# First unit of pairs 0 to 2: four of its eight transposed slots go through DRAM and VectorE instead of TensorE

## The reference

```python
hn = group_norm(x, gn1_scale, gn1_bias)
qkv = jnp.einsum('bchw,oc->bohw', hn, w_qkv) + b_qkv[None, :, None, None]
qkv = qkv.reshape(b * NHEAD, 3 * ch, n)
q, k, v = jnp.split(qkv, 3, axis=1)
scale = ch ** (-0.25)
wgt = jax.nn.softmax(jnp.einsum('bct,bcs->bts', q * scale, k * scale), axis=-1)
a = jnp.einsum('bts,bcs->bct', wgt, v).reshape(b, c, h, w)
out = jnp.einsum('bchw,oc->bohw', a, w_proj) + b_proj[None, :, None, None]
return x + group_norm(out, gn2_scale, gn2_bias)
```

## Time and profile before

| what | value |
|---|---|
| median of 3 runs | 3375.3 us (3374.86 to 3377.05) |
| the profiled execution, its own time | 3375.88 us |
| its span, first to last instruction | 3373.7 us |
| granted TensorE clock | 1.000 of full |
| PE busy | 3351.2 us, 99% |
| DVE, ACT, POOL busy | 63%, 55%, 32% |

### The profile page before, as it was taken

One profiled execution on the slowest core, in us unless ns is written; L12 is line 12 of the kernel. 1 busy time (PEld: TensorE's weight loads), 2 busy tenths in 40 slices (PEclk: granted clock), 3 DMA queues, 4 the chain that ended last, 5 costly groups with the idle time before them and its releaser, 6 DMA issues.

```text
span 3373.7 us, 51950 instructions
## 1 busy us (share of the span) xinstructions
PE 3351.2 (99%) x16816; PEld 2777.5 (82%) x16816; DVE 2132.7 (63%) x3489; ACT 1838.7 (55%) x3094; POOL 1064.3 (32%) x947
## 2 busy tenths in 40 slices
PE   8999999999999999999999999999999999999999
PEld 6888888888888888888888888888888888888887
DVE  5677357773578745786457854578555784557844
ACT  4677227862378523784337842388333882347822
POOL 1344104441045410453104531145211452124511
PEclk9999999999999999999999999999999999999999
DMA  8522244313534125331253212442224422343212
GB/s 340 149 67 59 79 131 124 93 34 94 140 99 101 62 57 151 103 86 76 53 167 91 73 75 76 144 101 63 93 61 144 98 63 94 92 139 70 63 57 75
DMA packets 109871, 332.15 MB, mean 98 GB/s; under 512 B 21760, under 2 KB 54784, under 8 KB 98816
## 3 DMA queue, kind: packets, MB, share of 16 engines
q1 hardware_dynamic: 107648, 322.15, 33.3%
q10 hardware_dynamic: 1920, 6.29, 0.9%
HBM read 162.68 MB, written 31.49 MB: 58 GB/s over the span
## 4 chain that ended last, share of the span: by engine, by line
PE 94%; DMA 2%; issue 1%; DVE 1%; SPq 1%; ACT 1%; POOL 0%; POOLq 0%; DVEq 0%
PE big L514 25%; PE big L648 14%; PE ops L634 14%; PE tps L619 14%; PE big L746 7%; PE big L655 5%; PE tps L819 5%; PE ops L819 5%; PE ops L598 3%; DMA ST<-ST 2%; PE tps L746 1%; SPq L419 0%; PE ops L746 0%; SPq L484 0%; PE ops L788 0%
## 5 line engine op out<-in xcount | busy, mean ns | idle before, releaser
L1097 POOL TENSOR_SCALAR PB<-PB,small 128x1024 f32<-128x1024 f32 x576 | 648.7, 1127 | 1294.8 <-DVE small L1342 1277.2
L1347 DVE TENSOR_TENSOR PT<-tps,PT 128x512 fp32r<-128x512 f32 x1024 | 652.5, 679 | 42.1 <-ACT PT L954 41.7
L1336 DVE TENSOR_REDUCE small<-big 128x1 f32<-128x1024 f32 x512 | 625.2, 1221 | 85.1 <-PE big L648 81.8
L954 ACT ACTIVATE PT<-tps 128x512 fp32r<-128x512 f32 x1024 | 564.1, 597 | 158.3 <-PE tps L619 155.4
L948 ACT ACTIVATE PB<-big,small 128x1024 f32<-128x1024 f32 x512 | 572.8, 1119 | 94.8 <-DVE small L1336 91.8
L634 PE MATMUL ops<-PT,VT 128*128 128x512 f32 x2048 | 599.1, 414 | 0.0
L648 PE MATMUL big<-ST 128*128 128x512 f32 x2048 | 554.2, 392 | 3.5 <-DMA ST<-ST 3.5
L619 PEld LDWEIGHTS tps<-ident,PB 128*128 128x128 f32 x4096 | 470.2, 140 | 95.4 <-DVE PT L1347 30.9
L619 PE MATMUL tps<-ident,PB 128*128 128x128 f32 x4096 | 545.7, 274 | 0.9
L648 PEld LDWEIGHTS big<-ST 128*128 128x128 f32 x2048 | 382.6, 188 | 91.5 <-issue 6.1
L634 PEld LDWEIGHTS ops<-PT,VT 128*128 128x128 f32 x2048 | 346.1, 189 | 47.1 <-DVE PT L1347 5.0
(11 more groups left out here) (188 smaller groups left out, 4911.7 us busy)
## 6 DMA issues: line engine op xcount, KB each, us to landing
ST<-ST SPq DMA_DIRECT2D x360, 256.0 KB, 5.3
W<-d_qk SPq DMA_DIRECT2D x32, 1024.0 KB, 7.0
W<-PB SPq DMA_DIRECT2D x256, 128.0 KB, 2.4
X<-in_x SPq DMA_DIRECT2D x8, 2048.0 KB, 10.2
W<-d_wp SPq DMA_DIRECT2D x8, 2048.0 KB, 11.9
W<-d_g SPq DMA_DIRECT2D x8, 2048.0 KB, 11.8
W<-d_m SPq DMA_DIRECT2D x8, 2048.0 KB, 7.7
W<-d_u SPq DMA_DIRECT2D x8, 2048.0 KB, 13.2
```

Of the source, the lines that this page charges most:

```text
L954: act_fn(pt_slot(u, s)[:, 0, :], tps[n % 2][:], ACT.Copy).then_inc(s_pt_hi, 1)
L1097: nc.gpsimd.tensor_scalar(PB[:, i, :], PB[:, i, :], rinv[:, i:i + 1], 1.0, ALU.mult, ALU.mult)\
L1336: V.tensor_reduce(negmax[:, i:i + 1], tile(("s", 4 * u + tb))[:], axis=AX.X, op=ALU.max, negate=True).then_inc(s_row_max, 1)
L1347: V.tensor_tensor(pt_slot(u, s)[:, 1, :], tps[n % 2][:], pt_slot(u, s)[:, 0, :].bitcast(f32), ALU.subtract).then_inc(s_pt_ready, 1)
```

## The change

For units 0, 4 and 8 (the first of pairs 0, 1 and 2; `MOVED`) slots 4 to 7, which are keys 512 to 1023, are no longer transposed by PE. SP stores each of the four row blocks' right half to DRAM (`d_e`, 128 x 512 words), once POOL has scaled it, and loads it back in 8 pieces of 32 partitions with runs of 128 words into X, which is free until the residual is loaded. DVE turns 32 x 32 blocks (`square`), two slots before and two after the rest of its step 7; ACT makes the high parts in steps 7 and 8 (`moved_hi`), POOL the low parts behind `normalise` 5 and 7 (`moved_lo`), and PE multiplies in steps 8 (slot 3), 9 (slots 4 and 5) and 10 (slots 6 and 7).

So that the runs are long, the right half of the keys of pairs 0 to 2 is written in another order: the key of slot s (of 4), block q and row r goes to column 128q + 4r + s (`keys_by_turn`). All four units of these pairs have this order, so in units 1 to 3, 5 to 7 and 9 to 11 PE transposes slots 4 to 7 with a step of 4 words between the keys that it reads.

Also: the parts of a projection go in the opposite order (keys before queries, right half first), in steps 5, 7, 8 and 10; X is loaded behind `stack_head(b, 3, 0)` and scaled in steps 50, 52, 54 and 56; and the first part of the output's copy (`corr`) of a moved unit comes a step later.

```diff
-QK_STEPS = (5, 7, 9, 11)
+QK_STEPS = (5, 7, 8, 10)
...
+MOVED = [4 * pair for pair in range(PAIRS - 1)]
+MOVED_SLOTS = [8 * u + s for u in MOVED for s in range(4, NT)]
...
+def transposed(step):
+
+    n = 2 * (step - LAG)
+    return [m for m in (n, n + 1) if m >= 0 and m not in MOVED_SLOTS]
+
+
+def valued(step):
+
+    n = 2 * (step - LAG) - 2
+    return [m for m in (n, n + 1) if m >= 0 and m not in MOVED_SLOTS and m + 1 not in MOVED_SLOTS[::4]]
+
+
+SQUARES_FIRST, SQUARES_LAST = {7: (4, 5)}, {7: (6, 7)}
+MOVED_HI = {7: (4, 5), 8: (6, 7)}
+MOVED_LO = {5: (4, 5), 7: (6, 7)}
+MOVED_VALUES = {8: (3,), 9: (4, 5), 10: (6, 7)}
...
-X_SCALE_STEPS = (20, 23, 26, 29)
+X_SCALE_STEPS = (50, 52, 54, 56)
...
+        F0 = X[:, 0:2, :].rearrange("p a (b n) -> p (a b) n", n=HALF)
+
+        def squared(s):
+
+            return X[:, 2 + (s - 4) // 2, HALF * (s % 2):HALF * (s % 2) + HALF]
...
+        def keys_by_turn(pair, half, row):
+
+            if half and 4 * pair in MOVED:
+                return row.rearrange("p (q r s) -> p s q r", q=QUARTERS, s=4)
+            return row.rearrange("p (s q r) -> p s q r", q=QUARTERS, s=4)
...
+            def move_quarters(b, u):
+
+                if u:
+                    sp.wait_ge(s_moved_lo, squared_count(b, 8 * (u - 4) + NT - 1))
+                    own_wait(sp)
+                for t in range(KB):
+                    sp.wait_ge(s_p_norm, b * 72 + 4 * u + t + 1)
+                    own_wait(sp)
+                    sp.dma_start(d_e[t], PB[:, t, HALF:N]).then_inc(s_moved_out[t // 2], 16)
+                for part in range(2):
+                    sp.wait_ge(s_moved_out[part], (b * len(MOVED) + MOVED.index(u) + 1) * 32)
+                    own_wait(sp)
+                    for q in range(QUARTERS):
+                        sp.dma_start(F0[32 * q:32 * q + 32, 2 * part:2 * part + 2, :],
+                                     d_e[2 * part:2 * part + 2].rearrange("t (q p) n -> p (t q) n", p=32)
+                                     [:, :, P * q:P * q + P]).then_inc(s_moved, 16)
+
...
-                sp.dma_start(X[:], src_x(b)).then_inc(s_x_res, 16)
...
+                move_quarters(b, 0)
...
+                move_quarters(b, 4)
                 stack_head(b, 2, 0)
                 stack_head(b, 2, 1)
...
+                move_quarters(b, 8)
                 stack_head(b, 3, 0)
+                sp.wait_ge(s_moved_lo, squared_count(b, MOVED_SLOTS[-1]))
+                own_wait(sp)
+                sp.dma_start(X[:], src_x(b)).then_inc(s_x_res, 16)
...
-                    pair, what, half = j // 4, j % 4 // 2, j % 2
+                    pair, what, half = j // 4, 1 - j % 4 // 2, 1 - j % 2
...
-                        pe.wait_ge(s_pt_ready, b * 144 + n - 1)
+                        bank_read = n - 2 if n - 2 not in MOVED_SLOTS else n - 6
+                        pe.wait_ge(s_pt_ready, pt_count(b, bank_read))
                     for t in range(4):
-                        last = nc.tensor.transpose(tps[n % 2][:, P * t:P * t + P],
-                                                   PB[:, 4 * (u % 2) + t, P * s:P * s + P], ident[:])
+                        row = PB[:, 4 * (u % 2) + t, :]
+                        if s >= 4 and u // 4 * 4 in MOVED:
+                            keys = row[:, HALF:N].rearrange("p (k s) -> p s k", s=4)[:, s - 4, :]
+                        else:
+                            keys = row[:, P * s:P * s + P]
+                        last = nc.tensor.transpose(tps[n % 2][:, P * t:P * t + P], keys, ident[:])
                     last.then_inc(s_t_full, 1)
...
+                    if n in MOVED_SLOTS:
+                        pe.wait_ge(s_moved_lo, squared_count(b, n))
+                    else:
+                        pe.wait_ge(s_pt_ready, pt_count(b, n))
...
+                    if n + 4 in MOVED_SLOTS:
+                        last.then_inc(s_values_read, 1)
...
+                    for m in of_moved(step, MOVED_VALUES):
+                        values0(m)
+                    for m in transposed(step):
+                        transposes(m // 8, m % 8)
+                    for m in valued(step):
+                        values0(m)
...
+                    to, of = unstacked(what, 0)[:, HALF * half:HALF * half + HALF], t[:, 0:HALF]
+                    if what:
+                        to, of = keys_by_turn(pair, half, to), of.rearrange("p (s q r) -> p s q r", q=QUARTERS, s=4)
+                    act_fn(to, of, ACT.Identity,
...
+                def moved_hi(n):
+                    act.wait_ge(s_squared, squared_count(b, n))
+                    act.wait_ge(s_values_read, b * len(MOVED_SLOTS) + MOVED_SLOTS.index(n) + 1)
+                    act_fn(pt_slot(n // 8, n % 8)[:, 0, :], squared(n % 8), ACT.Copy).then_inc(s_moved_hi, 1)
...
+                    for m in of_moved(step, MOVED_HI):
+                        moved_hi(m)
+                    for m in transposed(step):
+                        pt_hi(m // 8, m % 8)
...
+                def moved_lo(n):
+                    pool.wait_ge(s_moved_hi, squared_count(b, n))
+                    slot = pt_slot(n // 8, n % 8)
+                    nc.gpsimd.tensor_tensor(slot[:, 1, :], squared(n % 8), slot[:, 0, :].bitcast(f32), ALU.subtract)\
+                      .then_inc(s_moved_lo, 1)
+                    pool.wait_ge(s_moved_lo, squared_count(b, n))
...
+                    for m in of_moved(n, MOVED_LO):
+                        moved_lo(m)
...
+                def square(n):
+                    u, s = n // 8, n % 8
+                    if s == 4:
+                        dve.wait_ge(s_moved, (b * len(MOVED) + MOVED.index(u) + 1) * 32 * QUARTERS)
+                    V.transpose(squared(s).rearrange("p (t q r) -> p t q r", t=KB, q=QUARTERS),
+                                F0.rearrange("p t (q r s) -> p s t q r", q=QUARTERS, s=4)[:, s - 4, :, :, :])\
+                     .then_inc(s_squared, 1)
...
+                    for m in of_moved(step, SQUARES_FIRST):
+                        square(m)
...
+                    for m in of_moved(step, SQUARES_LAST):
+                        square(m)
+                    for m in transposed(step):
+                        pt_lo(m // 8, m % 8)
```

More of the change, by code:

```diff
@@ L46, in qk_part, with of_moved @@
     return None
+MOVED = [4 * pair for pair in range(PAIRS - 1)]
+MOVED_SLOTS = [8 * u + s for u in MOVED for s in range(4, NT)]
+def of_moved(step, table):
+    unit = 4 * (step // 16)
+    return [8 * unit + s for s in table.get(step % 16, ())] if unit in MOVED else []
+def transposed(step):
[8 more added lines that the diff above has]
+MOVED_VALUES = {8: (3,), 9: (4, 5), 10: (6, 7)}
 def a_parts(step):
@@ L104, in build @@
         d_r = nc.dram_tensor("d_r", [N], f32)
+        d_e = nc.dram_tensor("d_e", [KB, P, HALF], f32)
         X = sb("X", [P, KB, N])
@@ L233, in build @@
         s_ld_u = sem("ld_u")
+        s_moved_out = [sem(f"moved_out{i}") for i in range(2)]
+        s_moved = sem("moved")
+        s_squared = sem("squared")
+        s_moved_hi = sem("moved_hi")
+        s_moved_lo = sem("moved_lo")
+        s_values_read = sem("values_read")
         s_stack_a = sem("stack_a")
@@ L939, in qk_hi @@
                         act.wait_ge(s_stack_b, (b * PAIRS + pair) * 96)
-                    act_fn(unstacked(what, 0)[:, HALF * half:HALF * half + HALF], t[:, 0:HALF], ACT.Identity,
+                    to, of = unstacked(what, 0)[:, HALF * half:HALF * half + HALF], t[:, 0:HALF]
+                    if what:
+                        to, of = keys_by_turn(pair, half, to), of.rearrange("p (s q r) -> p s q r", q=QUARTERS, s=4)
+                    act_fn(to, of, ACT.Identity,
                            bias=(bq, bk)[what][:, pair:pair + 1])\
@@ L947, in exps @@
                     i = 4 * (u % 2) + tb
+                    if u - 2 in MOVED and tb == 0:
+                        for part in range(2):
+                            act.wait_ge(s_moved_out[part], (b * len(MOVED) + MOVED.index(u - 2) + 1) * 32)
                     act_fn(PB[:, i, :], t[:], ACT.Exp, bias=negmax[:, i:i + 1], accum_out=rowsum[:, i:i + 1])\
@@ L990, in body @@
                         qk_hi(qk_part(step))
-                    if n >= 0:
-                        pt_hi(n // 8, n % 8)
-                        pt_hi(n // 8, n % 8 + 1)
-                    if tb == 2 and u >= 2:
+                    for m in of_moved(step, MOVED_HI):
+                        moved_hi(m)
+                    for m in transposed(step):
+                        pt_hi(m // 8, m % 8)
+                    if tb == 2 and u >= 2 and u - 2 not in MOVED:
+                        corr(u - 2, 0)
+                    if tb == 3 and u - 2 in MOVED:
                         corr(u - 2, 0)
@@ L1324, in qk_lo @@
                 def qk_lo(j):
-                    pair, what, half = j // 4, j % 4 // 2, j % 2
+                    pair, what, half = j // 4, 1 - j % 4 // 2, 1 - j % 2
                     dve.wait_ge(s_big_hi, hi_count(b, ("qk", j)))
```

(19 more changed lines are left out.)

20 lines of the change are left out of this document (10 added, 10 removed).

## The result

The changed kernel takes **3385.2 us** (median of 10 runs, 3383.65 to 3387.56) against 3375.24 us before (10 runs, 3374.69 to 3377.8): a ratio of 1.0028 with an interval of 1.0018 to 1.0038. It is slower by 0.28%, some 10 us, where 3340 was forecast. The profiled execution has a span of 3384.6 us.

The account below looks back on a forecast made before the run. PE was taken to bound the kernel, busy 99% of the span with 94% of the chain. 3375.9 - 41.8 + 2 + 5 = 3341, rounded to 3340 us, range 3328 to 3402.

Parts of the forecast that it names:

- waits between parts: Steps 7 to 9: 0.15 us of PE wait twice a moved unit, less shorter transposes; net +2 us.
- squares: DVE's 32 x 32 turns: 0.87 us each, hidden in units 4 and 8, 0.3 us late in unit 0; +2 us.
- evictions of the reordered keys: ACT's and DVE's stepped writes: 0.3 us wait in each item's first round, otherwise hidden; +5 us together with squares.
- transposes that stay, step of 4 words: PE's 1152 remaining transposes reading the 4-word step: taken as zero extra, upper end +138 us.
- transfers: SP's stores and loads of moved blocks: hidden in both places, 0.8 us of margin in unit 0; zero.
- POOL: Four low parts of 1.29 us a unit fit in POOL's idle time, 0.6 us of margin in step 9; zero.
- What is removed: PE loses 16 transposes of 0.109 us in each of 24 moved units: -41.8 us.
- Rival 1, the step costs PE: Stepped reading lengthens PE's transposes: full price 3478 us (18%), partial 3350 to 3410 (12%); 30% in all.
- Rival 2, late loads: Loads of moved blocks land late before the squares, costing 61 us together, 3401 us; 12%.
- Rival 3, the change saves less: Squares at 1.22 us and slow evictions, or POOL late in step 9: 0.3 to 1.5 us a unit, 3350 to 3375; 8%.

Follow-up runs that it names:

- experiment 2: Changed kernel with only the evictions plain: 3369.7 us; with only the squares plain: 3382.17 us; kernel before with only 1536 transposes reading the 4-word step: 3387.77 us.
- experiment 1: Changed kernel with keys in plain order, so evictions, transposes and squares all use adjacent words: 3358.55 us.
- experiment 3: Changed kernel with as many stores and loads of the moved blocks, but carrying only 64 bytes a row: 3385.75 us.
- experiment 8: Changed kernel with keys in plain order and POOL reordering the moved units' right halves: 3360.28 us; the same with values spread over steps 7 to 10: 3347.97 us.
- Experiment 6: Kernel before with one transpose instead of four in each moved slot, 288 left out, all else kept: 3366.19 us.
- no_steps: The kernel of experiment 1: changed kernel with keys in plain order and no 4-word steps, 3358.55 us.
- experiment 7: Changed kernel with a moved unit's values spread over steps 7 to 10, two slots in each: 3376.49 us.
- experiment 9: `pool_reorders_spaced` with high parts behind step 8's exponential: 3348.99 us; with the last value low part later: 3345.37 us. POOL's reordering alone, parts in old steps: 3375.8 us.
- experiment 5: Kernel before with only the reordered keys: evictions and 1536 transposes use the 4-word step, nothing is moved: 3409.76 us.
- pool_reorders_spaced: Changed kernel with keys in plain order, POOL reordering the moved units' right halves, and values spread over steps 7 to 10: 3347.97 us.

## Why the prediction was wrong

The forecast was -41.8 (transposes) + 2 (waits between parts) + 5 (squares and evictions) = -35 us; measured is +10. The missing 45 us:

| term | forecast | measured | from |
|---|---|---|---|
| evictions of the reordered keys, squares | +5 | 15.5 + 3.0 | experiment 2 |
| transposes that stay, step of 4 words | 0 | about 9 | experiment 2 |
| waits between parts, with what was "removed" | -41.8 + 2 | -17.3 | experiment 1 |
| transfers, POOL | 0 | 0 | experiment 3, 8 |

The lines add up to +10.

**The steps that failed** are "Waits between parts in steps 7, 8 and 9" and "Evictions of the reordered keys".

*Waits between parts.* The mechanism was there: 1.51 us to empty a part against 1.38 us of PE's work. Its size was wrong. I counted the bare lateness, 0.15 us, twice a unit, and credited 0.2 for long transposes that go. The trace has both stops in every unit, with 0.17 us of lateness where the chain shows it (0.21 on average), and then a piece 0.3 us longer than usual. The row for it stood in my own working: the transposes behind a wait take 1.12 instead of 0.87. I read that as a wait of 0.25, and not as what any stop may add. At 0.47 us, two stops in each of 24 units are 22.6 us; with -41.8 that gives -19, and -17.3 was measured with all steps of 4 words gone. Behind it stands a broader error: I wrote that PE work that goes is time gained "as long as nothing is late in its place", and then entered all 41.8 us as gained, with 2 for what is late. Experiment 6 shows what that condition can be worth, 9.6 us of 31.4, though by another wait than the changed kernel's (`tps`, which is 2.4 us in `no_steps`): tiles change hands here with margins of tenths of a microsecond, and PE's shorter work uncovers them. Experiments 7, 8 and 9 show the same from the other side; each wait that goes uncovers another (`qk_lo`, then the exponential of step 8 before the projection, then before the scores).

*Evictions.* I had the right bounds (0.69 to 1.22; 1.14 and 1.18 measured, so the upper end), and covered them with "a whole step of 2.72 us to cover 1.51". That asked only when PE needs the reordered keys' tile. The 0.89 us that a reordered part adds on ACT and DVE also delays the maximum, the reciprocal and the `pt_lo` queued behind `qk_lo`; experiment 5's chain and the changed kernel's (992.66 to 998.14) both go through that. Of the 24 reordered parts the 8 at an item's start show no wait. The 16 in the rounds cost 15.5 us, 0.97 each, more than the 0.89 that they add, since each makes a stop: nothing was hidden, in the second round either, where the forecast had zero (step 22: PE idle 0.58 us, then 1.25 us instead of 0.87 for the transposes). The timeline of the first round, where my 0.3 us was to be, shows the size there (ACT, DVE and PE, steps 5 and 6):

```profile
936.46 1.18 ACT L1034 ACTIVATE ST<-big,vec 128x512 fp32r<-128x512 f32 x1 [0.39 <-PE big L595]
937.67 1.14 DVE L1447 SCALAR_TENSOR_TENSOR ST<-big,vec,ST 128x512 fp32r<-128x512 f32 x1 [2.85 <-ACT ST L1034]
938.87 1.21 PE L739 MATMUL big<-ST 128*128 128x512 f32 x4 [0.68 <-DVE ST L1447]
```

PE waits 0.68 us and then takes 1.21 instead of 0.92: 0.97 in all, the restart again.

**Point by point on the rest.** *What is removed*: 384 transposes went, at the price taken; only their worth was wrong. *Squares*: 1.075 us, inside the bounds, and 3.0 us in the whole, near the forecast's +2. The stall is where I had put it, in unit 0. DVE and ACT there, timeline:

```profile
944.77 2.06 DVE L1471 STREAM_TRANSPOSE X<-X 128x512 f32<-128x512 f32 x2
...
945.62 0.69 ACT L1034 ACTIVATE ST<-big,vec 128x512 fp32r<-128x512 f32 x1 [1.49 <-PE big L595]
946.76 0.71 DVE L1447 SCALAR_TENSOR_TENSOR ST<-big,vec,ST 128x512 fp32r<-128x512 f32 x1
```

The high part is done at 946.31, the squares end at 946.83 and `qk_lo` starts with them, 0.45 us late, eight times. *Transfers*: hidden in both places, as forecast. Timeline of SP and DVE in unit 4 (steps 21 to 23):

```profile
989.95 3.81 SPq L495 DMA_DIRECT2D X<-d_e  x8
...
999.72 2.07 DVE L1471 STREAM_TRANSPOSE X<-X 128x512 f32<-128x512 f32 x2
```

Eight loads are issued by 993.76; the page has 2.9 us for their landing, so they are there by 996.7 and the squares start at 999.72. In unit 0 they are issued from 935.70 to 939.51 and wanted at 944.77. The trace has no wait of DVE for the loads. *POOL*: busy for 126 us more (1190.5 against 1064.3), 0% of the chain. *Rival 1, the step costs PE*: its mechanism is real, at 0.0077 us on a transpose where it needed 0.031 to decide alone. The load of the stationary operand did grow, by some 0.07 us, but it lies beside the multiplication before it. The Trainium skill's "Advanced Engine Details and Errata", section Memory Cachelines, had the direction right on every engine that took such a step; the 1.04 us that I had estimated for a square from "Vector Engine (DVE) Microarchitecture Reference", section 5.2, whose figure is for a hop of 4 KiB and not of 4 words, is within 4% of the 1.075 measured, and the 129 us worked out from the same figure for PE are not there. The reading of "SBUF — State Buffer", section Door 1, by which four float32 are free, is contradicted by the evictions. *Rival 2, late loads*: did not happen. *Rival 3, the change saves less*: its causes, slow evictions above all, were the right kind, and I priced them at 0.3 to 1.5 us a unit; the whole loss against the forecast is 45 / 24 = 1.9 us a unit, 1.5 of it without the transposes' 9. 3385 lies within the range given, but by luck: the range reached that high for rivals 1 and 2; late loads did not happen, and PE's price for the step makes 9 of the 45 us.

Where the 0.3 us behind a stop lie, the timeline of the changed kernel shows (step 24):

```profile
1003.38 0.19 PEld L595 LDWEIGHTS big<-HH,W 128*128 128x128 f32 x1 [0.63 <-DVE ST L1447]
1003.38 0.50 PE L595 MATMUL big<-HH,W 128*128 128x512 f32 x1 [0.21 <-DVE ST L1447]
```

The load of the stationary operand waits too, and begins together with its multiplication, which then takes 0.50 us. In step 23, without a stop, it begins at 998.67, 0.23 us ahead of its multiplication, which takes 0.39. So the load is no longer hidden behind the work before it. What stays open is whether it could be: no run here lets it go ahead of the wait.

## What to carry to other kernels

Time taken off the busiest engine is worth only what the hand-overs around it leave: before counting it as gained, add up the shortest path by which each tile comes back, and price every stop with its restart (here 0.47 us for 0.17 of lateness), not with the lateness alone. When an instruction gets longer, ask not only who needs its result, but follow its engine's queue behind it until something is found that the bottleneck needs. A reordering belongs on an engine with slack (POOL here, within 2 us of no reordering at all), not in the order in which every producer and consumer must then step.

## What the runs showed of the hardware

A step of 4 float32 words costs ACT writing 512 words 1.18 us instead of 0.69, DVE writing and reading such a tile 1.14 instead of 0.75, and DVE's 32 x 32 transpose 1.075 instead of 0.69. On PE the load of a stationary operand of 128 such words takes up to 0.213 us instead of 0.140, and a chain of transposes only 0.01 us more each.

PE loses about 0.3 us behind each stop on top of the stop: projections of 3.00 to 3.03 us instead of 2.73, scores of 1.15 to 1.21 instead of 0.92, eight transposes of 1.25 to 1.35 instead of 0.87, where the load for the second four waits once more (0.18 us in step 22). It loses them even where it is hardly idle, when only the load of the stationary operand is held up (a projection of 3.02 us behind a load that waited 0.30, in `pool_reorders_spaced`).

Eight loads of 128 KB with 512 B packets were issued in 3.81 us, 0.48 each, and landed in 2.9 us (the page's median), faster than the 1 KB pieces of the exchange were issued (0.607 us each).
